# Edge attention of a graph network: matrix columns and edge weights read from PSUM, and another order of the work on PE and DVE

## What is computed

```python
for l in range(L):                      # L = 2
    xn = _layernorm(h, ln1_g[l], ln1_b[l])
    q = (xn @ wq[l] + bq[l]).reshape(n, H, DH)
    k = (xn @ wk[l] + bk[l]).reshape(n, H, DH)
    v = (xn @ wv[l] + bv[l]).reshape(n, H, DH)
    scores = jnp.einsum('ehd,ehd->eh', q[dst], k[src]) * scale
    m = jax.ops.segment_max(scores, dst, num_segments=n)
    ex = jnp.exp(scores - m[dst])
    z = jax.ops.segment_sum(ex, dst, num_segments=n)
    attn = ex / z[dst]
    agg = jax.ops.segment_sum(attn[:, :, None] * v[src], dst, num_segments=n)
    ...                                 # output product, second norm, feed-forward
```

## Time and profile before

| | us |
|---|---|
| median of 3 runs | 4388.59 |
| lowest, highest | 4388.18, 4395.11 |
| the profiled execution, its own time | 4386.98 |
| its span in the profile | 4385.3 |
| edge pass of layer one, from its full pace on | 341 to 1497 |
| edge pass of layer two, from its full pace on | 2274 to 3433 |

### The profile page before, as it was taken

How to read it: one execution, slowest core, us unless ns; L and a number is a source line. 1 busy time by engine, 2 the same in 40 slices (tenths; PEclk the granted TensorE clock), 3 DMA queues, 4 the chain that set the end, 5 groups by cost and what they waited for, 6 DMA issues and landing times. The chain is left out here.

```text
span 4385.3 us, 82262 instructions
## 1 busy us (share of the span) xinstructions
PE 3657.6 (83%) x17048; PEld 2421.9 (55%) x17048; DVE 3202.1 (73%) x7179; ACT 1681.7 (38%) x4755; POOL 2061.5 (47%) x1914
## 2 busy tenths in 40 slices
PE   1998889888898848999978898888889668888488
PEld 0654555555555427777755555555555337777377
DVE  4888999898989865555558898988899656666501
ACT  0114555555555502222225555555555302222022
POOL 2117777777777610000037777777777400000012
PEclk8999999999999979999989999999999879999699
DMA  3337777777777511111137777777777502222011
GB/s 72 120 112 220 217 217 220 212 216 211 215 215 218 173 62 48 48 60 60 48 118 211 214 219 211 218 213 209 212 219 220 165 22 75 84 78 78 26 46 39
DMA packets 357833, 640.42 MB, mean 146 GB/s; under 512 B 107755, under 2 KB 199981, under 8 KB 357594
## 3 DMA queue, kind: packets, MB, share of 16 engines
q0 software_dynamic: 140144, 457.44, 35.3%
q1 hardware_dynamic: 217610, 182.03, 14.1%
HBM read 570.14 MB, written 69.95 MB: 146 GB/s over the span
## 5 line engine op out<-in xcount | busy, mean ns | idle before, releaser
L673 POOL DMA_INDIRECT edge_kv<-kv,edge_idx x1664 | 1868.8, 1123 | 541.4 <-issue 416.9
L852 PE MATMUL edge_sums<-edge_kv,edge_sel 128*128 128x272 f32 x3328 | 982.9, 418 | 141.3 <-ACT edge_sums L920 111.8
L805 PE MATMUL edge_q<-qc,edge_spread 128*128 x3328 | 921.1, 400 | 153.1 <-DVE edge_kv L715 128.8
L919 ACT COPY acc<-edge_sums x1664 | 641.2, 385 | 869.5 <-PE edge_sums L852 699.2
L805 PEld LDWEIGHTS edge_q<-qc,edge_spread 128*128 128x128 f32 x3328 | 578.5, 191 | 431.6 <-issue 377.0
L852 PEld LDWEIGHTS edge_sums<-edge_kv,edge_sel 128*128 128x128 f32 x3328 | 567.5, 190 | 440.9 <-issue 363.1
L715 DVE TENSOR_TENSOR edge_kv<-edge_kv,edge_q 128x512 f32<-128x512 f32 x832 | 565.6, 680 | 242.9 <-DMA edge_kv<-kv,edge_idx 229.6
L920 ACT COPY edge_sums<-edge_blank 128x272 f32 x1664 | 659.7, 396 | 0.0
L764 DVE TENSOR_TENSOR edge_kv<-edge_kv 128x512 f32<-128x512 f32 x832 | 565.0, 679 | 0.8 <-ACT edge_kv L909 0.8
L722 DVE TENSOR_REDUCE edge_score<-edge_kv 128x16 f32<-128x512 f32 x832 | 560.0, 673 | 0.2
L758 DVE TENSOR_TENSOR edge_sel<-cols,edge_tab 128x256 f32<-128x256 f32 x832 | 340.3, 409 | 0.0
(11 more groups left out here) (369 smaller groups left out, 3912.1 us busy)
## 6 DMA issues: line engine op xcount, KB each, us to landing
edge_rel<-step_rel SPq DMA_DIRECT2D x208, 256.0 KB
edge_kv<-kv,edge_idx POOLq DMA_INDIRECT x1664, 3.9
edge_flags<-step_flags SPq DMA_DIRECT2D x416, 32.0 KB
picked<-last_picked SPq DMA_DIRECT2D x25, 513.0 KB
kv<-first_kv_out SPq DMA_DIRECT2D x25, 512.0 KB
kv<-middle_kv_out SPq DMA_DIRECT2D x25, 512.0 KB
end_rows<-edge_ends SPq DMA_DIRECT2D x416, 8.5 KB
h<-first_h SPq DMA_DIRECT2D x25, 256.0 KB
```

What stands on the lines that cost most here:

```text
L673: nc.gpsimd.indirect_dma_start(kv[:, turn[0], j, 0:KV], None, dram["kv"], bass.IndirectOffsetOnAxis(ap=idx[:, turn[0], j:j + 1], axis=0)). ...
L805: mm = t.matmul(psq[m % QBUFS][:, j % 2, :], spread[:, turn[0] % 2, j * P:(j + 1) * P], qc[:, bass.ds(at[j % 2], D)], start=True, stop=True)
L852: pe_p.tick(t.matmul(psa[:, bass.ds(place[j % 2], QC)], sel[:, j, :], kv[:, turn[0], j, D:ROW], start=False, stop=True, skip_group_check=T ...
L919: s.copy(acc[:, bass.ds(at, QC)], psa[:, bass.ds(bank, QC)])
```

## The change

- `cols` is copied once in a pass into the PSUM tile `turned`, and `sel` reads it there. ACT writes the exponentials into `turned` too (`psw`), and `value` reads them there; a second exponential of the same input (`kept`) writes the place in `kv` that the sums on PE read.
- All steps that touch `turned` are kept apart in time: DVE's `late 3` waits for `max_t` of the group after it (`follows`), and `tail 0` waits for the weights ahead of `sel`.
- `maxima` comes ahead of `below` on DVE. ACT tells of the weights as soon as they are in PSUM; PE's first pair of sums waits for `kept`.
- PE gets an order of its own, `PE_WEAVE`; DVE's `WEAVE` changes as well.

```diff
-WEAVE = (("product", 0), ("late", 2), ("score", 0), ("up", 0), ("product", 1), ("top", 0), ("late", 3),
-         ("score", 1), ("weigh", 0), ("product", 2), ("tail", 0), ("score", 2), ("product", 3), ("tail", 1),
+WEAVE = (("product", 0), ("score", 0), ("up", 0), ("late", 2), ("product", 1), ("top", 0), ("score", 1),
+         ("product", 2), ("late", 3), ("weigh", 0), ("score", 2), ("tail", 0), ("product", 3), ("tail", 1),
          ("score", 3), ("turn", 0))
+PE_WEAVE = (("product", 0), ("late", 2), ("top", 0), ("product", 1), ("product", 2), ("late", 3), ("tail", 0),
+            ("product", 3), ("turn", 0), ("tail", 1))
...
         pst = turned[0:G * H, 0:P]
         psm = turned[:, P:P + G * H]
+        psw = turned[:, P + G * H:P + 2 * G * H].rearrange("p (j h) -> p j h", h=H)
+        cols = turned[:, 512 - P:512]
...
-        dve_steps += ["up", "top", "below", "maxima"]
+        dve_steps += ["up", "top", "maxima", "below"]
...
-        act_p.begin(["weights"] + [f"acc{j}" for j in range(HALF)] + ["ends0"]
+        act_p.begin(["weights", "kept"] + [f"acc{j}" for j in range(HALF)] + ["ends0"]
...
+            v.tensor_copy(cols, keep["cols"][:, :]).then_inc(s_clear, 1)
...
+            def follows(turn):
+
+                if turn[1] is not None or turn != LAST_TURN:
+                    pe_p.wait(dve, later(turn, 1), "max_t")
...
                     if not earliest:
                         pe_p.wait(dve, later(turn, -1), f"sums{2 * m + 1}")
+                    if m == PAIRS - 1:
+                        follows(turn)
+                    if m == 0:
+                        act_p.wait(dve, turn, "weights")
                     at = 2 * m
-                    dve_p.tick(v.tensor_tensor(sel[:, at:at + 2, :], bc(keep["cols"][:, :].unsqueeze(1), [P, 2, P]),
+                    dve_p.tick(v.tensor_tensor(sel[:, at:at + 2, :], bc(cols.unsqueeze(1), [P, 2, P]),
                                                bc(tab[:, turn[0], 2 * m:2 * m + 2, 0:1], [P, 2, P]),
                                                ALU.is_equal), turn, f"sel{m}")
-                    if m == 0:
-                        act_p.wait(dve, turn, "weights")
                     values = kv[:, turn[0], 2 * m:2 * m + 2, D:KV].rearrange("p j (h d) -> p j h d", h=H)
                     dve_p.tick(v.tensor_tensor(values, values,
-                                               bc(kv[:, turn[0], 2 * m:2 * m + 2, KV:KV + H].unsqueeze(3), [P, 2, H, DH]),
+                                               bc(psw[:, 2 * m:2 * m + 2, :].unsqueeze(3), [P, 2, H, DH]),
                                                ALU.mult), turn, f"value{m}")
...
-                for what, m in WEAVE:
+                for what, m in PE_WEAVE:
...
                     if m > 0:
                         act_p.wait(pe, turn, f"acc{2 * m - 1}")
-                    elif not earliest:
-                        act_p.wait(pe, later(turn, -1), f"acc{G - 1}")
+                    else:
+                        act_p.wait(pe, turn, "kept")
+                        if not earliest:
+                            act_p.wait(pe, later(turn, -1), f"acc{G - 1}")
...
-                    act_p.tick(s.activation(kv[:, turn[0], :, KV:KV + H], below[:, :].rearrange("p (j h) -> p j h", h=H),
-                                            ACT.Exp, scale=SCALE), turn, "weights")
+                    less = below[:, :].rearrange("p (j h) -> p j h", h=H)
+                    act_p.tick(s.activation(psw, less, ACT.Exp, scale=SCALE), turn, "weights")
+                    act_p.tick(s.activation(kv[:, turn[0], :, KV:KV + H], less, ACT.Exp, scale=SCALE), turn, "kept")
```

More of the change, by code:

```diff
@@ L472, in is_first @@
     return turn[1] is None and turn[0] == 0 and turn[2] == 0
-CLEARED = 3
+CLEARED = 4
 def values_of(nc, engine, ap, most):
@@ L748, in rest @@
                     pe_p.wait(dve, turn, "max_t")
-                    dve_p.tick(v.tensor_tensor(below[:, :], score[:, lane, :], psm, ALU.subtract), turn, "below")
                     dve_p.tick(v.tensor_tensor(kv[:, turn[0], :, KV + H:ROW], psm.rearrange("p (j h) -> p j h", h=H),
@@ L752, in rest @@
                                turn, "maxima")
+                    dve_p.tick(v.tensor_tensor(below[:, :], score[:, lane, :], psm, ALU.subtract), turn, "below")
                 elif what in ("tail", "late"):
@@ L769, in _ @@
             groups_of(dve, body)
+            scan_up(LAST_TURN)
             rest(later(LAST_TURN, -1), "late", 2)
-            scan_up(LAST_TURN)
             rest(LAST_TURN, "top", 0)
```

## The result

The changed kernel takes 4448.84 us (median of 4 runs, 4446.5 to 4453.3), against 4388.39 of the kernel before run beside it (4 runs, 4372.47 to 4395.11): 1.0144 times as long, 95% interval 1.0116 to 1.0173. So it is slower by about 60 us, where 4337 was forecast and 4250 to 4405 was the range. The profiled execution took 4446.5 us with a span of 4444.7.

The account below looks back on a forecast made before the run. It took POOL as the bound before, PE together with ACT after: 11.07 + 0.10 = 11.17 us a group against 11.42, so 0.25 in each of 208 groups, 52 us off 4388.6, giving 4337 us; range 4250 to 4405.

Parts of the forecast that it names:

- PE's row of sums: Four pairs of sums in a group on PE, each waiting for ACT to empty the pair before; 11.07 us without address loads.
- Gathers released: On POOL: sel and value with one SBUF input each stop delaying gathers; from 11.41 to 10.0 to 10.4 us a group.
- sel and value no slower: On DVE: reading one input from PSUM costs these two instructions zero; the comparison was 680 against 679 ns.
- DVE keeps up: DVE's 10.32 us a group stays; it waits 0.6 us for max_t but is ahead by 0.6 to 1.5 us.
- The second Exp on ACT: One more exponential a group on ACT, covered by ACT's waiting for sums; 0.4 us a group if that cover went.
- Sums 3 to sums 0: Way on PE with only the ends between; the ACT loop decides: 2.59 us, PE idle 0.9.
- sums 0 to sums 1: Way on PE with a q pair and score_t between, about 2.2 of work; the ACT loop decides: 2.59 us.
- Sums 1 to sums 2: Way on PE with sums, ends and one q pair, 2.57 us, plus 0.09 for the loop's turn: 2.66 us.
- Sums 2 to sums 3: Way on PE with sums, max_t and two q pairs in a row: 2.87 to 3.46 us, taken as 3.23.
- 0.10 for the loads: Two address loads in a row between PE's two q pairs would delay PE by 0.10 us a group.
- The slow rival: PE starves at two address loads ahead of the next group's q0: 0.60 us a group, 4441 us; chance 0.17.
- POOL's 11.41 us: POOL's period for a group before the change, 8 x (1.121 + 0.305), without waiting for anybody; taken as the bound.

Follow-up runs that it names:

- the exchanged kernel: The changed kernel with PE's steps product 2 and late 3 exchanged, and sel and value reading SBUF again: 4239.31 us, ratio 0.9662 to the kernel before.

## Why the prediction was wrong

The place was named: PE's row of sums, bound by PE together with ACT after POOL is let go. The failure is the size of one term and what was made of it.

- **Gathers released: right.** 0.961 us was measured, "near 0.95 to 1.0" said; POOL waits up to 2.7 us. sel and value no slower: value 675 ns, where the earlier trace rows have 679 (341 to 1497).

```profile
L776 DVE TENSOR_TENSOR edge_kv<-edge_kv,edge_turned 128x512 f32<-128x512 f32 x390 | 263.1, 675 | 0.0
```

- **DVE keeps up: right.** 56.6 us in 96 waits for max_t are 0.59 each; 0.6 was said. Two waits of DVE that were not forecast, 31.6 us in 95 for the scores' transpose and 42.0 in 88 for q, still leave it idle time: it is busy for 1014 of 1156 us. The second Exp on ACT shows nowhere in the waits (its price was read as 0.39 where the earlier trace rows have 0.40, which changes nothing).
- **Sums 3 to sums 0, sums 0 to sums 1: right. Sums 1 to sums 2: a little short.** In the rows above they are 2.55, 2.55 and 2.65 against 2.59, 2.59 and 2.66, and PE's waits for ACT 0.80 and 0.36 against 0.8 and 0.3. Over all groups, the turn of the loop included, the means are 2.58, 2.60 and 2.80: the third was 0.14 short.
- **Sums 2 to sums 3: wrong.** 3.23 and 0.10 for the loads were taken; 3.67 and 4.04 stand above, and 3.77 is the mean. The step that failed is "If every group had the mean one it would be 0.29, and in most groups there is none: I take 0.10". With one load moved out, all else as forecast, the kernel takes 4327 us, 10 us from the 4337 of the forecast: the second load accounts for the rest, 122 us or 0.59 a group, where 0.10 was taken. The mean way from sums 2 to sums 3 is then 3.21, where 3.23 was taken without loads. That the total comes so near is in part luck: the 0.10 for loads and the 0.14 missing from sums 1 to sums 2 nearly cancel.
- **Why that term was so small.** It came from idle rows of PE, where a load shows only if nothing hides it, and before, sums or ends stand ahead of nearly every one. The load has rows of its own, which the sum does not use; in the trace of before, 341 to 1497:

```profile
L482 PEldq TENSOR_LOAD <-edge_regs_q x406: 532/545/962, 343.0 to 1496.8; - x136
L482 PEldq TENSOR_LOAD <-edge_regs_s x403: 532/544/826, 348.0 to 1496.0; - x135
```

Two loads are 1.09 us against a q pair of 1.03, and by the rows of the changed kernel the queue needs 0.3 to 0.6 us more (1.40 and 1.69 from q pair to q pair). So the second load can't be hidden there: 0.4 to 0.7 us open up ahead of the second q pair. The Trainium skill, page "DMA: Bandwidth & Descriptors", section "Latency and other measured facts", gives a `tensor_load` floor of about 600 ns; here the shortest is 532 and the median 545. That two loads in a row already stand behind the ends, hidden, was true, but the ends and the sums give 1.68 us of cover, and the q pair gives 1.0.
- **The slow rival** was this very mechanism, at 4441 us; 4449 was measured. It had 0.17, and the range was cut at 11.5 us a group although its own bounds reached 11.81, which is 4470 us. The bounds held, the cut did not.
- **What bounded the kernel before** was read only half. POOL was the engine without a pause and DVE waited for rows, but the same operands run at 4229 us with both orders matched. So POOL's 11.41 us was not fixed by the operands, as the step "a gather stands still until a DVE instruction with two inputs in SBUF has left" had it, and more than the forecast's gain was there to be had without PSUM.

## What to carry to other kernels

Where an order is rewritten, list for each engine what its queue issues between two blocks of work, register loads too, price them from their own rows, and ask what is still running in front of them; idle time of the engine prices only what was not hidden so far. Engines whose orders were tuned to each other are to be changed together: here each half alone lost 1.4% to 1.9% and both won 3.8%. An engine without any pause is not yet the bound: look whether its consumer waits.

## What the runs showed of the hardware

A load of two addresses into registers takes 0.545 us of PE's queue. One such load is hidden behind a q pair worth 1.0 us; each further one costs 0.57 to 0.59 us a group.

How long DVE holds gathers up is no constant of the operands: with the same SBUF operands the mean gather took 1.030 us in groups of 10.67 us (the exchanged kernel: 792 gathers in 1056 us), 1.121 in groups of 11.39, and in the kernel with DVE alone in the new order (341 to 1397):

```profile
L676 POOL DMA_INDIRECT edge_kv<-kv,edge_idx x714 | 840.6, 1177 | 217.6 <-issue 188.1 <-PE edge_sums L855 21.3 <-PE edge_end_sums L866 8.2
```

It is 1.177 us, 8 x (1.177 + 0.305) = 11.86 us, again without a pause above 0.3 us, although DVE hardly waits for rows there and PE and DVE wait for each other:

```profile
POOL edge_kv L676 <- issue: 188.1, 617, 0.3
...
DVE edge_kv L718 <- DMA edge_kv<-kv,edge_idx: 14.0, 22, 2.2
```

In all three POOL has no pause above 0.3 us, whatever the group takes. That gathers slide against DVE's steps until they are held up just long enough would explain it; no run shows this, and it stays open, as does what share of the 11.41 us of before was POOL's own.
